# Reordered TensorE fillers between the turned-block runs of a fused attention and mixture-of-experts kernel

## What is computed

```python
x = L0_attn_x                        # (8, 512, 128), float32
xn = _layernorm(x, axis=-1)
# attention: 16 heads of 8 columns, causal, scores minus log1p(decay * log1p(distance))
scores = jnp.einsum('bhqd,bhkd->bhqk', q, k) * (1.0 / jnp.sqrt(jnp.float32(D)))
att = jax.nn.softmax(scores + attn_mask[None], axis=-1)
y = jnp.einsum('bhqk,bhkd->bhqd', att, v)          # then @ w_proj
# experts: 8 experts of 512 hidden columns, the best 2 per token, silu
x = x + _L0_attn_ref(xn, ...) + _L0_ffn_ref(xn, ...)
```

## Time and profile before

| | |
|---|---|
| time, median of 3 runs | 533.34 us (532.91 to 533.88) |
| the profiled execution's own time | 531.52 us |
| its span, first to last instruction | 529.1 us |
| mean granted TensorE clock | 0.976 |
| TensorE matmul busy | 480.2 us, 91% |
| TensorE weight load busy | 349.7 us, 66% |
| VectorE busy | 363.0 us, 69% |
| ScalarE busy | 319.9 us, 60% |
| GpSimd busy | 361.4 us, 68% |
| DMA, mean | 152 GB/s |

### The profile page before, as it was taken

One profiled execution on the slowest core, in us unless ns is written; L12 is line 12 of the kernel. 1 busy time (PEld: TensorE's weight loads), 2 busy tenths in 40 slices (PEclk: granted clock), 3 DMA queues, 4 the chain that ended last, 5 costly groups with the idle time before them and its releaser, 6 DMA issues.

```text
span 529.1 us, 13373 instructions
## 1 busy us (share of the span) xinstructions
PE 480.2 (91%) x4316; PEld 349.7 (66%) x4316; DVE 363.0 (69%) x1406; ACT 319.9 (60%) x568; POOL 361.4 (68%) x598
## 2 busy tenths in 40 slices
PE   6777999989999999999999999999999999999920
PEld 5544556555565665565565565565999999999920
DVE  7596987988988878888879879872433333333326
ACT  4578767777877878878877878766233333333300
POOL 3875565556999999987899899891355555555524
PEclk9979999999999999999999999999999999999985
DMA  6566691580460451450461451365466766667349
GB/s 179 171 221 215 172 221 29 157 215 8 136 185 18 140 169 35 140 161 25 138 172 32 137 169 47 94 187 131 125 197 200 209 211 208 207 186 226 113 164 322
DMA packets 71825, 80.37 MB, mean 152 GB/s; under 512 B 8638, under 2 KB 52672, under 8 KB 71760
## 3 DMA queue, kind: packets, MB, share of 16 engines
q1 hardware_dynamic: 67440, 71.06, 46.2%
q0 software_dynamic: 4320, 8.47, 4.5%
HBM read 48.11 MB, written 31.84 MB: 151 GB/s over the span
## 4 chain that ended last, share of the span: by engine, by line
PE 70%; DVE 21%; POOL 3%; DMA 2%; issue 2%; ACT 1%; SPq 0%; DVEq 0%; ACTq 0%; POOLq 0%
PE psT L1291 21%; DVE scores L1121 13%; PE psO L1309 13%; PE ps L1336 12%; PE psT L1363 12%; PE ps L1266 7%; PE psM L1250 2%; POOL xn_all L734 2%; DVE x_all L535 2%; PE ps L1327 1%; DVE xn_all L959 1%; PE psM L1320 1%; POOL rstd L727 1%; DMA probs<-picked_dram 1%; ACT probs L884 1%
## 5 line engine op out<-in xcount | busy, mean ns | idle before, releaser
L1121 DVE CUSTOM_DVE_ANT_0 scores<-ps,wdist 128x256 f32<-128x256 f32 (+3 forms) x512 | 218.4, 486 | 26.9 <-PE ps L1266 24.3
L765 POOL TENSOR_SCALAR scores<-scores,row_max 128x384 f32<-128x384 f32 (+3 forms) x416 | 200.4, 496 | 43.1 <-DVE row_max L1121 41.6
L884 ACT ACTIVATE probs<-psT 128x512 f32<-128x512 f32 x320 | 173.8, 595 | 67.2 <-PE psT L1291 67.2
L1291 PE MATMUL psT<-ident,scores 128*128 128x128 f32 x1280 | 175.8, 280 | 3.7 <-ACT probs L884 3.2
L1291 PEld LDWEIGHTS psT<-ident,scores 128*128 128x128 f32 x1280 | 136.3, 140 | 63.9 <-issue 42.6
L783 POOL DMA_INDIRECT picked_dram<-scores,row_ring x71 | 69.8, 983 | 79.2 <-DVE scores L1173 77.8
L893 ACT ACTIVATE scores<-ps 128x512 f32<-128x512 f32 x71 | 42.4, 597 | 93.8 <-PE ps L1336 93.8
L1309 PE MATMUL psO<-probs,values 128*32 128x512 f32 (+3 forms) x1024 | 82.0, 438 | 0.0
L1336 PE MATMUL ps<-scores,wdist 128*128 128x128 f32 x568 | 75.3, 276 | 0.8 <-DVE scores L1161 0.8
L1363 PE MATMUL psT<-wdist,scores 128*128 x568 | 75.0, 275 | 0.0
L776 POOL DMA_INDIRECT rows_dram<-xn_all x64 | 63.3, 989 | 16.4 <-issue 16.4
(11 more groups left out here) (140 smaller groups left out, 279.3 us busy)
## 6 DMA issues: line engine op xcount, KB each, us to landing
wdist<-w1t SPq DMA_DIRECT2D x71, 256.0 KB, 3.3
k_rows<-k_dram SPq DMA_DIRECT2D x64, 96.0 KB, 2.8
q_rows<-q_dram SPq DMA_DIRECT2D x64, 96.0 KB, 2.6
row_ring<-rows_dram SPq DMA_DIRECT2D x71, 65.0 KB, 3.1
probs<-picked_dram SPq DMA_DIRECT2D x8, 512.0 KB, 6.5
rows_dram<-row_ring SPq DMA_DIRECT2D x7, 585.0 KB, 5.7
k_dram<-k_parts SPq DMA_DIRECT2D x7, 384.0 KB, 2.4
q_dram<-q_parts SPq DMA_DIRECT2D x7, 384.0 KB, 2.6
```

Source lines behind the costliest of these rows:

```text
L765: last = nc.gpsimd.tensor_scalar(part, part, -1.0, row_max[:, r, tile, quad:quad + 1], ALU.mult, ALU.add)
L884: nc.scalar.activation(probs[:, at.ring(2), w, :], psT[:, w % 2], ACT.Exp, scale=-1.0).then_inc(exp_ready, 1)
L1121: last = nc.vector.tensor_tensor_reduce(out=scores[:, r, u, col:col + n], in0=bank[:, col:col + n], in1=wdist[:, at.g * QUADS + quad, SEQ ...
L1291: last = nc.tensor.transpose(psT[:, w % 2, place * P:(place + 1) * P], scores[:, at.ring(2), u, col + key * P:col + (key + 1) * P], ident[:])
```

## The change

In the list of each slot the score steps and value products change places around the five turned runs. The order becomes S0 S1, T0, S2, T1, V01, T2, S3 S4, T3, V23, T4. No step is added or taken away. Because all engines walk the same list, VectorE's and GpSimd's parts of the score steps move too, against `KR`, `QR`, `PJ`, `KL` and `QL`.

```diff
     step("SA", n, NGROUP, (0, 1))
-    step("PV", n - 2, NGROUP, 0)
-    step("PV", n - 2, NGROUP, 1)
+    p1(2)
     per_batch("KR", -3)
     per_batch("QR", -2)
     step("TE", n - 1, NGROUP, 2, 4)
+    step("PV", n - 2, NGROUP, 0)
+    step("PV", n - 2, NGROUP, 1)
     per_batch("KM", -3)
     per_batch("QM", -2)
...
-    p1(2)
+    step("TE", n - 1, NGROUP, 4, 6)
     p1(3)
-    step("TE", n - 1, NGROUP, 4, 6)
+    p1(4)
     per_batch("KL", -3)
     per_batch("QL", -2)
+    step("TE", n - 1, NGROUP, 6, 8)
     step("PV", n - 2, NGROUP, 2)
     step("PV", n - 2, NGROUP, 3)
-    step("TE", n - 1, NGROUP, 6, 8)
     per_batch("KW", -3)
     per_batch("QW", -2)
     per_batch("XT", -4)
-    p1(4)
     step("TE", n - 1, NGROUP, 8, 10)
```

## The result

The changed kernel takes 541.19 us (median of 4 runs, 539.81 to 543.03) against 533.12 for the kernel before (4 runs on the same chip, 531.22 to 533.88): a ratio of 1.0167, 95% interval 1.0144 to 1.0189. It is slower by 1.7%, 8.1 us. The profiled execution took 543.03 us, the longest of the four; its span is 540.6 us, its mean granted clock 0.971.

What follows compares the result with a forecast made beforehand. TensorE was taken to set the pace, its pieces end to end with 0.36 us avoidable a slot. Slots 9 to 28 +6.9, slots 1 to 8 +2.2, slots 29 to 31 0: +9.1 on 533.34, thus 542.4 us, range 537.0 to 546.0.

Steps and rivals of the forecast that it cites:

- S1's gap and T4's filler: In each slot on TensorE, 0.27 us before S1 and 0.09 before T4 would go: 0.36 a slot, 1.44 a round.
- S2's waits: S2 on TensorE waits for VectorE's S0: 0, 0.82, 0.32 and 1.07 us in key, query, projection and plain slots.
- d: Time from S0's issue until VectorE begins it: 0.53 us when idle, 1.89 in query slots, 1.28 in plain ones.
- T3 behind `QM`: In query slots `QM` waits for `QR`, now behind S2 on VectorE, so T3 comes 0.6 us late.
- The round: Four slots (key, query, projection, plain): waits of 2.81 less 1.44 give +1.37, thus 41.3 us; five rounds +6.9.
- Slots 1 to 8: Early slots, where VectorE was already late through the routing: +2.2 us, bounds 0 and 4.
- a clock below 1.00: A granted clock below 1.00 in the slots, listed as a sign of being wrong: waits would cost more than their length.
- Slots 29 to 31: Slots without `KA` or `QA`: between -0.1 and +0.6 us, taken as 0.
- bounds of 4 to 13 us: Total slowdown with the early slots at their ends; the forecast's own range was given as 538.0 to 546.0 us.
- the faster rival: S2 does not wait and the 0.36 us a slot stay gained, GpSimd giving about 2 back: 524 us; chance 6%.
- The other: Nothing changes: VectorE or GpSimd sets the slots and TensorE's order is no matter, 533.3 us; chance 5%.

Runs made afterwards that it cites:

- kernel 1: The changed kernel with `KR` and `QR` put back ahead of S2 on VectorE; median 536.67 us, ratio 1.0067 to the kernel before.
- Kernel 8: The changed kernel with the new order in slots 9 to 31 only, the old one in slots 0 to 8; 538.71 us, ratio 1.0102 to the kernel before.
- kernel 9: The changed kernel with the new order in slots 0 to 8 only, the old one behind them; 536.50 us, ratio 1.0044 to the kernel before.
- Kernel 4: The kernel before with its value products spread, one filler between every two runs, score steps left in place; 529.12 us, ratio 0.9943.
- kernels 1 to 3: The changed kernel with `KR` and `QR` ahead of S2, with `OT` behind the next slot's S0, and with both: 536.67, 538.34 and 531.43 us.
- kernel 7: Kernel 4 with GpSimd's unit 7 of each group given to ScalarE, units 6 and 7 behind T3's exponentials; 525.84 us, ratio 0.9876 to the kernel before.
- kernel 6: The kernel before with only S2 and V01 moved (and S3 behind T2), S4 left alone ahead of T4; 553.10 us, ratio 1.0362.

## Why the prediction was right

The median forecast was 542.4 us, 9.1 above the kernel before; measured were 541.19, 8.1 above it. By its steps:

- **S1's gap and T4's filler, -0.36 in a slot:** the key slot shows 10.20 less 9.81, 0.39.
- **S2's waits** were to be 0, 0.82, 0.32 and 1.07; they were 0, 0.67, 0.33 and 0.97. VectorE began S0 at d = 1.73 where 1.89 was forecast, in the query slot, and at 247.09 - 245.90 = 1.19 where 1.28 was, in the plain one. I had let it begin S3 0.53 behind its issue, as S0; it began it 0.43 behind (221.59 and 242.94 for 221.16 and 242.52), and `OT` ahead of the query slot took 1.47 instead of 1.54.
- **T3 behind `QM`, 0.6:** it was 0.63, and kernel 1 took it away alone.
- **The round, +1.37:** +1.13 measured, so five rounds +5.5 where +6.9 were forecast. Kernel 8 puts the price of slots 9 and on at 5.4 us.
- **Slots 1 to 8, +2.2:** kernel 9 shows 2.3, and its slots 2 to 8 took 77.12 us where 77.3 were worked out, each of the seven within 0.2 of its own figure. In the changed kernel's profile they cost 4.94. Most of the difference is the clock, a term that the sum did not have: I had named a clock below 1.00 only as what would prove me wrong, and by that sign it was wrong for this execution. It was the longest of the four, 11.5 us over the profile of before, and there the rounds that had been put too high and the missing clock term work against each other. The median does not need that term: 5.5, 2.3 and 0.1 give 7.9 of its 8.1 us. The forecast is 1 us above it because the rounds were put 1.4 too high.
- **Slots 29 to 31, 0:** +0.14.

The profiled span grew by 540.6 - 529.1 = 11.5 us, 0.9 of it behind slot 31 (368.28 - 357.73 = 10.55 at its end). That is in the expert blocks, which took 515.3 - 378.9 = 136.4 us from the first silu pass to the last for 135.6 before. The change does not touch them, and kernel 9's 139.9 shows that they vary more than that between executions.

Two sums of the prediction do not come out. Its bounds of 4 to 13 us are 537.3 to 546.3, not 538.0 to 546.0. And the time of the faster rival was put too low: 22 slots in which GpSimd takes 9.92 us for TensorE's 9.6 would give back up to 7 us, not 2, thus up to 529 and not 524. Neither moves the forecast.

The two rivals fell as argued. The faster one needed VectorE to be done with S0 at 1.43; it began S0 at 1.73 in the query slot. The other held TensorE's order to be free. Kernel 4 moves nothing but value products, which only TensorE works on, and is 0.6% faster; kernels 1 to 3, which add and remove no piece of work, are up to 1.8% faster than the change, by the waits ahead of TensorE's pieces. By the Trainium skill (Perfetto Trace Analysis, Identifying the Most-Contended Engine) TensorE's headroom is to be judged by the share of peak flops that it reaches and by its weight loads, not by its matmul rows. The weight loads are 23.48 of 39.15 us in kernel 7's round; GpSimd's 29.95 and VectorE's 33.99 would stand before them. As a sign of what binds, the measurement speaks against the weight loads in this kernel: the starts that stand end to end told it.

## What to carry to other kernels

Where an engine's pieces stand end to end, follow each shared bank around its cycle (issue, the reader's start, the reader's end) before a piece is moved: a reader that is late by a fixed amount is hidden by what stands between, and an order that cuts this distance (here from over 4 us to 1.57) pays for every small step ahead of the reader. Before giving such an order up, move the small steps: two of them here turned a loss of 1.7% into a gain of 0.2%. And look at the granted clock behind every new idle time of TensorE, since it can cost as much again.

## What the runs showed of the hardware

- After idle times of 1.02 to 1.56 us ahead of a piece, TensorE's granted clock fell in some cases from 1.00 to 0.50 (from 2.4 to 1.2 GHz) and rose again, mostly within 4 us, for 1.2 to 1.6 us lost where a run and V01 follow. In others, with the same idle time at the same place, it stayed: behind 1.34 in three of the seven slots of kernel 6 that have it, behind 1.34 and 1.57 in kernel 9, and behind 1.02 in the kernel before where kernel 7 fell. No fall stood behind the 0.92 us of the plain slots in the changed kernel. What decides it these runs do not show.
- The expert blocks, the same work in the same order at full clock, took 135.6, 136.4 and 139.9 us from the first silu pass to the last in three profiled executions (before, changed kernel, kernel 9).
- The products of V01 cost 1.64 us in one run of matmuls and 1.78 in two pieces with other steps between them (kernel 4). Why was not tried.
- VectorE began `OT` 0.61 behind `KL`, whose row has a length of 0.69: chains are better summed by starts than by lengths.
